# Attention sums of a graph layer: two of sixteen tiles weighted on VectorE, rows loaded two rounds ahead

## The chip, the cores and the metric
The kernel runs on one core of a Trainium2 chip. The metric is the device time of one execution in microseconds (us). The engines are TensorE (PE in the profile; its weight loads are PEld), VectorE (DVE), ScalarE (ACT), GpSimd (POOL) and SyncE (SP), which issues DMAs. Each engine runs its own stream of instructions in order; they meet only at semaphores, counters that an instruction raises when it is done and that another engine waits for.

## What is computed
Four layers follow one another on a graph of 3125 nodes and 53125 directed edges (sorted by their destination): graph attention, a mixture of experts, a five-layer graph convolution, and a second mixture of experts. The change touches one stage of the graph attention only, its last three lines:

```
h = (x @ W.T).reshape(n, H, D)                 # H = 8 heads of D = 32
h_src = h[src]
alpha = (h_src . a_src) + (h_dst . a_dst) + (enc . h_dst), leaky relu 0.2
ex = exp(alpha - segment_max(alpha, dst)[dst])
attn = ex / segment_sum(ex, dst)[dst]
out = segment_sum(h_src * attn[..., None], dst)   # this stage
return out.reshape(n, H * D) + bias
```

So every edge's row of 256 numbers (8 heads of 32) is multiplied by that edge's 8 attention weights, and the weighted rows of all edges with the same destination are added up.

## The kernel before
The stage is the function attention_sums. Edges are handled in tiles of 128 (one edge for each partition); there are 416 tiles, in 26 rounds (ITERS) of 16 tiles (BODY). Tile j of a round goes through four steps, on four engines, and SP feeds them:

- **SP, rows (L885) and weights (L888).** The gathered rows of the edges lie in DRAM (e_rows). They come in quads of four tiles, 544 KB each, into at_g, which has room for one round. Quad v of the next round is loaded as soon as the four tiles of quad v of this round are weighted (semaphore weighted). The attention weights at_attn come in halves of a round, two rounds ahead.
- **POOL, product (L878).** at_msg = row times weight, 128x256, both operands and the result in SBUF. It waits for the rows, for the weights, and, before each even tile, for summed: the slot of at_msg (sixteen of them) must have been read by PE one round earlier. Each product raises weighted.
- **ACT, one-hot (L936, L941).** It builds for each tile the 128x128 matrix that says which edge goes to which node of a window of 128 nodes, a quad at a time.
- **PE, sums (L959).** Per pair of tiles: wait for the one-hots (hot), for both products (weighted), and for added, that is, DVE has taken over the results that lie in the same PSUM bank from one round earlier (there are eight banks, one for each pair). Then two 32-bit matmuls for each tile, each of which stands as two in the profile, so eight for a pair. The pair raises summed by 2.
- **DVE, adds (L975).** add_tile adds the 128x256 result of a tile from PSUM to the window of agg that starts at the tile's first node. Successive windows overlap, so each add waits for summed and also for added: the add before it must have finished. DVE works four tiles (LAG) behind the tile number of its loop. The function body handles one round; its first act is lagging_bases, which loads the sixteen window starts into registers (L162, L163). The first round is written out (`body(0, True)`), the other 25 are a loop of one round (L985, `dve.Fori(1, ITERS)`), and the last four adds are written out behind the loop.

PE is thus held by three rings of sixteen tiles: at_msg between POOL and PE, the one-hots between ACT and PE, and the PSUM banks between PE and DVE. The stages before and behind this one are separated from it by a barrier of all engines.

## Time and profile before
| | us |
|---|---|
| median of 3 runs | 4766.83 (4765.92 to 4767.99) |
| the profiled execution's own time | 4765.28 |
| its span (first to last instruction) | 4763.5 |
| this stage in it, first row load to last add | 706.5 to 1002.0 |

| engine | busy us | share of the span |
|---|---|---|
| PE | 3822.2 | 80% |
| PEld | 3231.1 | 68% |
| DVE | 3018.3 | 63% |
| POOL | 2904.6 | 61% |
| ACT | 2211.9 | 46% |

The shares are means over stages that differ widely, so they say little about one stage. The stage of the change is 6% of the span; of its lines the page lists POOL's product at 242.4 us busy (416 of them, 614 ns each), PE's matmuls at 236.8 us (1664, 292 ns each; they overlap), and DVE's adds at 175.6 us (416, 422 ns each). Busy time is that of the instructions; waiting and register work of an engine's sequencer is not in it. Which engine sets the pace has to be read from the order of the waits in the stage.

### The profile page before, as it was taken

Reading aid. Unit: us, or ns where it says so; the run is one execution under the profiler, and the core shown is the slowest. Engines: PE = TensorE matmul, PEld = TensorE weight load, DVE = VectorE, ACT = ScalarE, POOL = GpSimd, SP = SyncE. Lnnn points to the kernel's source line nnn. Section 1 sums busy time; section 2 is a strip of 40 time slices with the busy share of each in tenths; the row PEclk is TensorE's granted clock in tenths of the full one; section 3 lists DMA queues with packets and bytes.
Section 4 is the critical chain, followed back from the end, with each engine's and each line's share of the span. In section 5 each row is a group of like instructions: output and inputs, shape, how many; then the busy total and the mean of one; then the engine's idle time right before and its main releaser. Section 6 shows DMA issues by size and latency. Waiting matters only on the chain. (4 is left out here: it accounts for less than half of the span.)

```text
span 4763.5 us, 103541 instructions
## 1 busy us (share of the span) xinstructions
PE 3822.2 (80%) x21812; PEld 3231.1 (68%) x21813; DVE 3018.3 (63%) x7234; ACT 2211.9 (46%) x4854; POOL 2904.6 (61%) x3160
## 2 busy tenths in 40 slices
PE   6999908867999688878888778886888878887598
PEld 4666607756888577767777677775777767776465
DVE  5667676664222576776776767776777767777544
ACT  3222227632232356555565555564556546565221
POOL 3777709823333477766777477774777747776142
PEclk8999959968999899999999899998999989999599
DMA  6888828735665555554555455553555535554432
GB/s 216 252 255 255 246 72 233 209 96 190 191 203 144 158 158 164 160 152 141 162 161 162 132 154 161 158 166 125 161 158 165 163 124 158 164 159 138 136 119 70
DMA packets 401352, 784.98 MB, mean 165 GB/s; under 512 B 178781, under 2 KB 242385, under 8 KB 383657
## 3 DMA queue, kind: packets, MB, share of 16 engines
q1 hardware_dynamic: 256115, 409.00, 26.7%
q0 software_dynamic: 133728, 352.78, 26.0%
q10 hardware_dynamic: 11094, 19.50, 1.3%
q14 instruction: 378, 3.10, 0.2%
q8 instruction: 37, 0.61, 0.1%
HBM read 665.35 MB, written 113.43 MB: 163 GB/s over the span
## 5 line engine op out<-in xcount | busy, mean ns | idle before, releaser
L2450 POOL DMA_INDIRECT g_g<-xl_rows,src_all x1640 | 1557.7, 950 | 525.9 <-issue 427.5
L2475 PE MATMUL g_b<-g_we,g_ea 128*128 128x256 f32 x4160 | 1163.5, 404 | 427.9 <-DVE g_msg L2575 372.7
L2488 PEld LDWEIGHTS g_b<-g_onehot,g_msg 128*128 128x128 f32 x8320 | 1117.0, 197 | 120.7 <-DVE agg L2596 36.7
L2488 PE MATMUL g_b<-g_onehot,g_msg 128*128 128x128 f32 x8320 | 1138.0, 281 | 36.7 <-DVE agg L2596 22.0
L2475 PEld LDWEIGHTS g_b<-g_we,g_ea 128*128 128x128 f32 x4160 | 734.7, 197 | 577.2 <-DVE g_msg L2575 461.7
L2596 DVE TENSOR_TENSOR agg<-agg,g_b 128x256 f32 x2080 | 870.0, 418 | 284.3 <-issue 145.5
L2552 ACT ACTIVATE g_msg<-g_msg 128x512 f32<-128x512 f32 x1040 | 652.8, 628 | 790.7 <-DVE g_msg L2575 784.7
L2575 DVE TENSOR_TENSOR g_msg<-g_g,g_b 128x512 f32<-128x512 f32 x1040 | 712.2, 685 | 402.9 <-DMA g_g<-xl_rows,src_all 239.2
L2532 ACT ACTIVATE g_away<-iota_row,dst_rel 128x128 f32<-128x128 f32 x1040 | 406.0, 390 | 209.2 <-DMA g_g<-xl_table,src_all 134.9
L2450 POOL DMA_INDIRECT g_g<-xl_table,src_all x410 | 390.8, 953 | 166.3 <-issue 153.8
L521 POOL DMA_INDIRECT sc_g<-h_table,sc_idx x416 | 405.2, 974 | 133.0 <-issue 116.7
L2537 ACT ACTIVATE g_onehot<-g_away,pos_w,neg_w 128x128 f32<-128x128 f32 x832 | 410.5, 493 | 110.8
L553 PE MATMUL sc_pe_h<-ae_h_rows,sc_onehot 128*128 x1664 | 429.4, 402 | 39.3 <-DVE sc_prod L658 39.3
L553 PEld LDWEIGHTS sc_pe_h<-ae_h_rows,sc_onehot 128*128 128x128 f32 x1664 | 301.5, 191 | 127.1 <-issue 85.6
L2582 DVE TENSOR_SCALAR g_onehot<-iota_row,dst_rel,pos_w 128x128 f32<-128x128 f32 x832 | 299.0, 359 | 83.9 <-issue 62.9
L878 POOL TENSOR_TENSOR at_msg<-at_g,at_attn 128x256 f32<-128x256 f32 x416 | 242.4, 614 | 140.3 <-DMA at_g<-e_rows 109.8
L596 ACT ACTIVATE sc_enc<-sc_pe_e 128x512 f32<-128x512 f32 x208 | 118.8, 598 | 425.8 <-PE sc_pe_e L542 398.2
L959 PE MATMUL at_ps<-at_onehot,at_msg 128*128 128x128 f32 x1664 | 236.8, 292 | 84.4 <-POOL at_msg L878 41.5
L959 PEld LDWEIGHTS at_ps<-at_onehot,at_msg 128*128 128x128 f32 x1664 | 209.2, 200 | 111.9 <-POOL at_msg L878 86.5
L1958 POOL DMA_INDIRECT sum_d<-ex_y,ex_give x56 | 100.0, 1787 | 266.3 <-DVE ex_y L1915 160.2
L1869 ACT ACTIVATE ex_hid<-ex_hp,ex_b 128x256 f32<-128x256 f32 (+1 forms) x256 | 114.4, 447 | 301.6 <-PE ex_hp L1827 297.7
L975 DVE TENSOR_TENSOR agg<-agg,at_ps 128x256 f32 x416 | 175.6, 422 | 120.2 <-PE at_ps L959 79.5
(359 smaller groups left out, 4298.5 us busy)
## 6 DMA issues: line engine op xcount, KB each, us to landing
g_ea<-in_ea SPq DMA_DIRECT2D x260, 512.0 KB
ex_w<-in_f_w SPq DMA_DIRECT2D x80, 1024.0 KB, 6.6
e_rows<-sc_g SPq DMA_DIRECT2D x52, 1088.0 KB, 5.0
at_g<-e_rows SPq DMA_DIRECT2D x104, 544.0 KB, 4.6
g_fetched<-xl_rows SPq DMA_DIRECT2D x3072, 1.0 KB
g_g<-xl_rows,src_all POOLq DMA_INDIRECT x1640
sc_rel<-rel_row ACTq DMA_DIRECT2D x52, 256.0 KB, 4.9
g_fetched<-xl_table SPq DMA_DIRECT2D x768, 1.0 KB
```

Source lines behind the costliest of these rows:

```text
L521: nc.gpsimd.indirect_dma_start(out=g[:, j, :], out_offset=None, in_=k.h_table[:, :], in_offset=bass.IndirectOffsetOnAxis(ap=idx[:, q, j % ...
L553: last = nc.tensor.matmul(pe_h[u % HB][:, i, 0:HROW], onehot[:, q, b, (at + i) * P:(at + i + 1) * P], k.h_rows[:, bass.ds(blocks[2 * u + i ...
L959: last = nc.tensor.matmul(ps[u][:, at:at + P], msg[:, j, b * P:(b + 1) * P], onehot[:, j, :], start=True, stop=True)
L2450: nc.gpsimd.indirect_dma_start(out=g.g[:, j, 0:width], out_offset=None, in_=table[:, :], in_offset=bass.IndirectOffsetOnAxis(ap=k.src_all[ ...
L2475: last = nc.tensor.matmul(ep[u % EB][:, i * D:(i + 1) * D], g.ea[:, q, (at + i) * P:(at + i + 1) * P], g.we[:], start=True, stop=True)
L2488: last = nc.tensor.matmul(ps[u % (SB // 2)][:, at:at + P], g.msg[:, j, b * P:(b + 1) * P], g.onehot[:, j, :], start=True, stop=True)
L2532: nc.scalar.activation(g.away[:, j // 2 % 2, :], k.iota_row[:], ACT.Abs, bias=k.dst_rel[:, bass.ds(it * BODY + j, 1)], scale=-1.0).then_in ...
L2537: nc.scalar.activation(g.onehot[:, j, :], g.away[:, j // 2 % 2, :], ACT.Relu, bias=bias, scale=scale).then_inc(g.act_hot, 1)
L2552: nc.scalar.activation(m, m, ACT.Relu).then_inc(g.relu, 1)
L2575: nc.vector.tensor_tensor(g.msg[:, 2 * u:2 * u + 2, :], g.g[:, 2 * u:2 * u + 2, 0:D], ep[u % EB][:, 0:2 * D].rearrange("p (a d) -> p a d", ...
L2582: nc.vector.tensor_scalar(g.onehot[:, j, :], k.iota_row[:], k.dst_rel[:, at], weight, ALU.is_equal, ALU.mult).then_inc(g.hot, 1)
L2596: nc.vector.tensor_tensor(window, window, ps[u % (SB // 2)][:, i * D:(i + 1) * D] .rearrange("p (b n) -> p b n", b=K), ALU.add).then_inc(g ...
```

## The change
DVE takes over the product of tiles 4 and 12 of every round (BY_DVE); POOL does the other fourteen and skips these two. DVE does such a product eight tiles (V_AHEAD = HALF) ahead of the tile number of its loop: tile 12 at the start of loop step j = 4, and tile 4 of the next round at step j = 12; since its adds lag by four tiles, tile 12 is weighted just before the add of tile 0 of the same round, and tile 4 of the next round just before the add of tile 8. Each product on DVE waits for its rows, its weights and its slot of at_msg (summed), and raises a new semaphore by_dve, for which PE (at the pairs that hold tiles 4 and 12) and SP wait besides weighted.

at_g gets room for two rounds instead of one, with eight semaphores for the landed quads instead of four, and SP loads both first rounds at once, then always two rounds ahead. SP's stream is written out in full instead of being a loop. DVE's loop now has two rounds in its body; the first two rounds and the last two are written out, so eleven turns of two rounds remain.

```diff
--- before.py
+++ after.py
@@ -854,60 +854,64 @@
     nc, a = k.nc, k.a
     PAIRS, QUADS = BODY // 2, BODY // 4
     ROUNDS = 2
+    BY_DVE = (4, 12)
+    ON_POOL = BODY - len(BY_DVE)
+    V_AHEAD = HALF
+
+    def of_pool(j):
+        return j - sum(t < j for t in BY_DVE)
+
+    def of_dve(j):
+        return sum(t < j for t in BY_DVE)
+
     with ExitStack() as c:
         sem, sb, bank = makers(k, c, "at")
-        g = sb("g", [P, BODY, GROW])
+        g = sb("g", [P, ROUNDS, BODY, GROW])
         attn = sb("attn", [P, ROUNDS, BODY, HEADS])
         msg = sb("msg", [P, BODY, D])
         onehot = sb("onehot", [P, BODY, P])
         one = sb("one", [P, 1])
         away = sb("away", [P, 2, 4, P])
         ps = [bank(f"ps{u}") for u in range(PAIRS)]
-        rows_in = [sem(f"rows_in{v}") for v in range(QUADS)]
+        rows_in = [sem(f"rows_in{v}") for v in range(ROUNDS * QUADS)]
         attn_in = [sem(f"attn_in{n}") for n in range(2 * ROUNDS)]
-        weighted, unit, distance, hot, summed, added = map(sem, (
-            "weighted", "unit", "distance", "hot", "summed", "added"))
+        weighted, by_dve, unit, distance, hot, summed, added = map(sem, (
+            "weighted", "by_dve", "unit", "distance", "hot", "summed", "added"))
         block = c.enter_context(nc.Block())
 
         def rows_of(it, v):
 
             return k.e_rows[bass.ds(it, 1), :, 4 * v:4 * v + 4, :].rearrange("a p t c -> p (a t) c")
 
-        def product(r, j):
-
-            return nc.gpsimd.tensor_tensor(
-                msg[:, j, :].rearrange("p (h c) -> p h c", h=HEADS), head_cols(g[:, j, 0:HROW]),
+        def product(engine, r, j):
+
+            return engine.tensor_tensor(
+                msg[:, j, :].rearrange("p (h c) -> p h c", h=HEADS), head_cols(g[:, r, j, 0:HROW]),
                 attn[:, r, j, :].unsqueeze(2).broadcast_to([P, HEADS, HD]), ALU.mult)
 
         @block.sync
         def _(sp):
-            def load_rows(v, it):
-                sp.dma_start(g[:, 4 * v:4 * v + 4, :], rows_of(it, v)).then_inc(rows_in[v], 16)
+            def load_rows(r, v, it):
+                sp.dma_start(g[:, r, 4 * v:4 * v + 4, :], rows_of(it, v)).then_inc(rows_in[r * QUADS + v], 16)
 
             def load_attn(r, q, it):
                 sp.dma_start(attn[:, r, q * HALF:(q + 1) * HALF, :], tile_rows(k.attn_d, it * BODY + q * HALF, HALF)
                              ).then_inc(attn_in[2 * r + q], 16)
 
-            load_attn(0, 0, 0)
-            load_rows(0, 0)
-            load_rows(1, 0)
-            load_attn(0, 1, 0)
-            load_rows(2, 0)
-            load_rows(3, 0)
-            for q in range(2):
-                load_attn(1, q, 1)
-            with sp.Fori(0, ITERS // ROUNDS - 1) as turn:
-                for r in range(ROUNDS):
-                    it = turn * ROUNDS + r
-                    for v in range(QUADS):
-
-                        sp.wait_ge(weighted, it * BODY + 4 * (v + 1))
-                        load_rows(v, it + 1)
-                        if v % 2 == 1:
-                            load_attn(r, v // 2, it + ROUNDS)
-            for v in range(QUADS):
-                sp.wait_ge(weighted, (ITERS - 2) * BODY + 4 * (v + 1))
-                load_rows(v, ITERS - 1)
+            for r in range(ROUNDS):
+                for v in range(QUADS):
+                    if v % 2 == 0:
+                        load_attn(r, v // 2, r)
+                    load_rows(r, v, r)
+            for it in range(ITERS - ROUNDS):
+                r = it % ROUNDS
+                for v in range(QUADS):
+                    sp.wait_ge(weighted, it * ON_POOL + of_pool(4 * (v + 1)))
+                    if of_dve(4 * (v + 1)):
+                        sp.wait_ge(by_dve, it * len(BY_DVE) + of_dve(4 * (v + 1)))
+                    load_rows(r, v, it + ROUNDS)
+                    if v % 2 == 1:
+                        load_attn(r, v // 2, it + ROUNDS)
 
         @block.gpsimd
         def _(pool):
@@ -916,12 +920,13 @@
                     it = turn * ROUNDS + r
                     for j in range(BODY):
                         if j % 4 == 0:
-                            pool.wait_ge(rows_in[j // 4], it * 16 + 16)
+                            pool.wait_ge(rows_in[r * QUADS + j // 4], turn * 16 + 16)
                         if j % HALF == 0:
                             pool.wait_ge(attn_in[2 * r + j // HALF], turn * 16 + 16)
                         if j % 2 == 0:
                             pool.wait_ge(summed, it * BODY + j + 2)
-                        product(r, j).then_inc(weighted, 1)
+                        if j not in BY_DVE:
+                            product(nc.gpsimd, r, j).then_inc(weighted, 1)
 
         @block.scalar
         def _(act):
@@ -951,7 +956,9 @@
                     v = u // 2
                     if u % 2 == 0:
                         pe.wait_ge(hot, it * QUADS + u // 2 + 3)
-                    pe.wait_ge(weighted, it * BODY + 2 * u + 2)
+                    pe.wait_ge(weighted, it * ON_POOL + of_pool(2 * u + 2))
+                    if 2 * u in BY_DVE or 2 * u + 1 in BY_DVE:
+                        pe.wait_ge(by_dve, it * len(BY_DVE) + of_dve(2 * u + 2))
                     pe.wait_ge(added, it * BODY + 2 * u + 2)
                     for j in (2 * u, 2 * u + 1):
                         for b in range(K):
@@ -975,15 +982,39 @@
                 nc.vector.tensor_tensor(window, window, ps[j // 2][:, j % 2 * D:(j % 2 + 1) * D]
                                         .rearrange("p (b n) -> p b n", b=K), ALU.add).then_inc(added, 1)
 
-            def body(it, first):
+            def weight_tile(turn, r, j):
+
+                it = turn * ROUNDS + r
+                dve.wait_ge(rows_in[r * QUADS + j // 4], turn * 16 + 16)
+                dve.wait_ge(attn_in[2 * r + j // HALF], turn * 16 + 16)
+                dve.wait_ge(summed, it * BODY + j - j % 2 + 2)
+                product(nc.vector, r, j).then_inc(by_dve, 1)
+
+            def weight_ahead(turn, r, j, final):
+
+                wraps, at = divmod(j + V_AHEAD, BODY)
+                if at in BY_DVE and not (final and wraps):
+                    of_turn, of_round = (turn, r) if r + wraps < ROUNDS else (turn + 1, -ROUNDS + r)
+                    weight_tile(of_turn, of_round + wraps, at)
+
+            def body(turn, r, first, final=False):
+                it = turn * ROUNDS + r
                 bases = lagging_bases(k, dve, base_regs, it * BODY)
                 for j in range(BODY):
+                    weight_ahead(turn, r, j, final)
                     if j >= LAG or not first:
                         add_tile(it * BODY + j - LAG, (j - LAG) % BODY, bases[j])
 
-            body(0, True)
-            with dve.Fori(1, ITERS) as it:
-                body(it, False)
+            for j in range(V_AHEAD):
+                if j in BY_DVE:
+                    weight_tile(0, 0, j)
+            for r in range(ROUNDS):
+                body(0, r, r == 0)
+            with dve.Fori(1, ITERS // ROUNDS - 1) as turn:
+                for r in range(ROUNDS):
+                    body(turn, r, False)
+            for r in range(ROUNDS):
+                body(ITERS // ROUNDS - 1, r, False, r == ROUNDS - 1)
             for i, base in enumerate(lagging_bases(k, dve, base_regs[0:LAG], ET)):
                 add_tile(ET - LAG + i, BODY - LAG + i, base)
             dve.wait_ge(added, ET + BODY)
```

## Rows read from the trace of the kernel before

**Rows 1.** Windows: start:end and length, then each engine's busy us (and count).
```profile
core 0: us, PE busy (x) PEld busy (x) DVE busy (x) ACT busy (x) POOL busy (x), PEclk, DMA share, GB/s
707.00:747.00 40.00, 34.44 (x240) 30.71 (x240) 19.36 (x46) 35.26 (x94) 36.25 (x64) 0.88 0.94 261
747.00:989.50 242.50, 200.12 (x1408) 176.57 (x1408) 147.82 (x351) 160.99 (x426) 206.20 (x353) 0.96 0.75 203
```

**Rows 2.** Waits of 712 to 1002.1: who waited for whom, us in total, times, longest.
```profile
PEld at_ps L959 <- POOL at_msg L878: 86.5, 54, 39.9
DVE agg L975 <- PE at_ps L959: 79.5, 145, 8.0
...
PE at_ps L959 <- DVE agg L975: 37.1, 22, 1.7
POOL at_msg L878 <- PE at_ps L959: 30.5, 28, 1.7
```

**Rows 3.** Timeline of DVE, loop: start, length, what, times [idle before].
```profile
754.30 0.98 DVE L975 TENSOR_TENSOR agg<-agg,at_ps 128x256 f32 x2 [0.20 <-PE at_ps L959]
757.17 0.98 DVE L975 TENSOR_TENSOR agg<-agg,at_ps 128x256 f32 x2 [1.89 <-PE at_ps L959]
```

**Rows 4.** Timeline of PE and of POOL, 843 to 862.
```profile
847.04 9.36 PE L959 MATMUL at_ps<-at_onehot,at_msg 128*128 128x128 f32 x64 [1.74 <-DVE agg L975]
...
848.25 9.41 POOL L878 TENSOR_TENSOR at_msg<-at_g,at_attn 128x256 f32<-128x256 f32 x16 [1.68 <-PE at_ps L959]
```

**Rows 5.** Timeline of POOL, 700 to 762.
```profile
710.75 51.69 POOL L878 TENSOR_TENSOR at_msg<-at_g,at_attn 128x256 f32<-128x256 f32 x90 [109.81 <-DMA at_g<-e_rows]
```

**Rows 6.** Timeline of DVE, adds outside the loop: first round, then the last.
```profile
714.21 0.42 DVE L975 TENSOR_TENSOR agg<-agg,at_ps 128x256 f32 x1 [8.01 <-PE at_ps L959]
...
715.91 0.42 DVE L975 TENSOR_TENSOR agg<-agg,at_ps 128x256 f32 x1 [0.65 <-PE at_ps L959]
...
717.42 0.42 DVE L975 TENSOR_TENSOR agg<-agg,at_ps 128x256 f32 x1 [0.47 <-PE at_ps L959]
...
721.78 0.42 DVE L975 TENSOR_TENSOR agg<-agg,at_ps 128x256 f32 x1 [0.20 <-PE at_ps L959]
723.83 0.98 DVE L975 TENSOR_TENSOR agg<-agg,at_ps 128x256 f32 x2 [1.63 <-PE at_ps L959]
...
999.75 0.42 DVE L975 TENSOR_TENSOR agg<-agg,at_ps 128x256 f32 x1 [0.47 <-DVE agg L975]
1000.37 0.42 DVE L975 TENSOR_TENSOR agg<-agg,at_ps 128x256 f32 x1 [0.20 <-DVE agg L975]
```

**Rows 7.** Line L162 (register loads), 715 to 990: count, ns min/median/max.
```profile
L162 DVEq TENSOR_LOAD <-base_lag x25: 1097/1102/1139, 722.0 to 988.3; - x25
```

**Rows 8.** Timeline of DVE: L1651 has two SBUF operands.
```profile
4539.41 0.42 DVE L1651 TENSOR_TENSOR ex_y<-ex_y,ex_xr 128x256 f32<-128x256 f32 x1
4539.75 0.42 DVE L1644 TENSOR_TENSOR ex_y<-ex_yp,ex_b 128x256 f32<-128x256 f32 x1
```

**Rows 9.** Timeline of DVE in a later stage: a free instruction behind adds.
```profile
2501.42 0.97 DVE L2596 TENSOR_TENSOR agg<-agg,g_b 128x256 f32 x2
2502.30 0.34 DVE L2582 TENSOR_SCALAR g_onehot<-iota_row,dst_rel,pos_w 128x128 f32<-128x128 f32 x1
```

**Rows 10.** Timeline of DVE and POOL, 4491 to 4495: two SBUF operands on both.
```profile
4491.17 0.33 DVE L1442 TENSOR_TENSOR st_hi_hot<-iota_row,st_hi 128x160 f32<-128x160 f32 x1
...
4492.31 0.59 POOL L1430 TENSOR_TENSOR st_value<-st_hi_hot,weight 128x160 f32<-128x160 f32 x1 [6.44 <-DVE st_lo_hot L1444]
4492.51 0.58 DVE L1442 TENSOR_TENSOR st_hi_hot<-iota_row,st_hi 128x160 f32<-128x160 f32 x1
```

**Rows 11.** Line L885, issues of 706 to 709.28: count, ns, and landing times.
```profile
L885 SPq DMA_DIRECT2D at_g<-e_rows x4: 424/560/580, 706.5 to 708.7; - x4
...
DMA to landing us min/median/max: 4.0/5.4/7.3
```

**Rows 12.** Timeline of PEld in a later stage: one pair of tiles, no wait.
```profile
2503.22 1.08 PEld L2488 LDWEIGHTS g_b<-g_onehot,g_msg 128*128 128x128 f32 x8
```

## The prediction

> **What bounds the stage now.** Read first the windows of the stage [rows 1]. In the long middle stretch (747 to 989.5 us) PE is busy 200 of 242 us, POOL 206, DVE 148: by busy time DVE comes last. The waits [rows 2] seem to agree: the largest sum is PE's weight loads waiting for POOL's products, 86.5 us. Both readings mislead, and the timelines show why. PE sits idle 1.74 us once a round, and what ends it is an add of DVE at the ring of PSUM banks; POOL then sits idle 1.68 us, ended by PE [rows 4]. So POOL waits for PE, and PE for DVE. DVE has the same gap, 1.89 us once a round [rows 3]; it is put down to PE, but PE had summed that tile long before (it is a ring of sixteen tiles ahead and itself waits for the next add). In this gap DVE's sequencer jumps back in its loop and loads sixteen window starts into registers, 1.10 us each time, 25 times [rows 7].
>
> DVE's beat is a chain: an add may start only when the one before it is done. Two adds take 0.98 us, so the second starts 0.55 us after the first, and the next pair starts 1.17 to 1.18 us after this one, which leaves 0.62 us between the pairs [rows 3]. Eight pairs are 9.4 us, and the step from a round's last add (754.85) to the next round's first (757.17) is 2.32 us in place of 0.62. Round: 9.4 + 1.7 = 11.1 us. POOL alone needs 51.69/90 = 0.574 us a tile, which it held until 762 us without a stop [rows 5], or 9.2 us a round; a pair on PE without a wait needs about 1.1 us at most [rows 12], or 8.6 us. DVE is the bound from its first add at 714.21 on, with only two short waits for PE in the first round [rows 6]. Whatever is put on DVE lengthens the stage, unless it fits into a gap of the chain; what is taken from POOL is taken from slack.
>
> **The parts of the change.**
>
> *POOL's two products fewer.* 2 x 0.574 us a round from an engine that already waits: worth 0.
>
> *DVE's two products more, the chain.* Such an instruction (both operands in SBUF, 256 numbers) lasts 0.42 us, and the next independent one starts 0.34 us after it [rows 8]. It always stands before an even tile, so in the 0.62 us step. It doesn't wait for the add in front of it, and it can start before that add has left the engine: a later stage has a free instruction 0.33 us after an add's start (the second add starts at 2501.97, the other at 2502.30) [rows 9]. Then product and next add are at 0.34 and 0.68 us: 0.06 more than 0.62. That is the low end. The three waits with their register work that the product brings along stand in front of it on DVE's sequencer; if they end only 0.1 us after the add is over, the next add starts at 0.42 + 0.1 + 0.34 = 0.86: 0.24 more, the high end. I take 0.15, nearer to the middle since some of that work fits under the running add. 50 products (52 less the two of the start, below) x 0.15 = 7.5 us (3 to 12).
>
> *The same, against POOL.* In a later stage DVE and POOL both run products with SBUF operands [rows 10]. L1442 takes 0.33 us alone; started at 4492.51, while POOL's L1430 ran from 4492.31 to 4492.90, it takes 0.58 and ends 0.19 us behind POOL's end. DVE was held until POOL had finished. DVE's adds read one operand from PSUM and show nothing of this: 0.42 us beside a POOL that never rests. The Trainium skill (SBUF — State Buffer, section "SBUF: two separate sides") says that VectorE instructions with two SBUF inputs and GpSimd instructions that read SBUF take one shared port pair in turns, for a whole instruction at a time. The trace agrees with it (0.58 against 0.33 us); that rule speaks against this change, since a product on POOL and one on DVE can't run side by side, and it makes the hold that I price here a standing cost rather than an accident.
>
> How often does it bite? PE can't pass tile 12 before DVE has weighted it, so PE now runs in bursts of four pairs: from product 12 to tile 4 of the next round, and so on. Let product 12 end at time 0. PE sums its pairs by about 1.1, 2.1, 3.1, 4.1 us [rows 12]; POOL, released by each of them, works from 1.2 to 1.8 and then from 2.2 to 5.7 us (six products at 0.574). DVE does eight adds (4.7 us) and comes with its next product at about 4.4: POOL is in the middle of one. The wait is what is left of it, between 0 and 0.5 us, and I take 0.25. In the other half round DVE has the round's end as well, comes at about 6 us, and finds POOL at rest. So 25 x 0.25 = 6.3, and 0.7 for the first three rounds, in which POOL never rests [rows 5]: 7 us (0 to 25 if all fifty waited 0.5).
>
> *Start.* DVE's first add (714.21) now stands behind product 12 of round 0, which needs the last quad. That quad was issued at 708.7 and took up to 7.3 us to land [rows 11]: 716.0. Plus 0.1 (an estimate) for the semaphore, 0.34 for the product, 0.25 for POOL: first add at 716.7, 2.5 us later. The two waits for PE that DVE then no longer meets were (0.65 - 0.20) + (0.47 - 0.20) = 0.7 us [rows 6]. Net +1.8 (0 to 3). If that quad lands later because eight are now asked for at once, this grows; they are queued behind it, so I add nothing.
>
> *DVE's loop of two rounds.* A step between rounds that is written out or lies inside the body has no jump: 723.83 - 721.78 = 2.05 us [rows 6] in place of 2.32. Of the 25 such steps, 24 were jumps and 10 will be: 14 x 0.27 = 3.7 us less (2 to 5). Against that, adds that are written out stand 0.62 us apart, each of them (1000.37 - 999.75) [rows 6], where every second one in the loop took 0.55. 48 more tiles are written out: 24 x 0.07 = 1.7 us more.
>
> *Rows two rounds ahead, SP written out.* POOL waited for rows once, at the start [rows 5]; nothing later hangs on them, so they are worth 0. They are also what keeps DVE from waiting: DVE needs tile 12's rows while the slot of the round before may still be in use. With one room DVE would meet that wait; with two, SP is released by DVE's product a round and a half before DVE needs the rows, some 17 us, against a landing of 7.3 at most [rows 11]. PE's and SP's new wait for by_dve: PE stops there once in each half round, as above, with the loads and matmuls of the following pair queued behind it; DVE is then eight adds from wanting them. Five more semaphores to clear behind the stage: 0.1 us, left out.
>
> **Sum.** 1.8 + 7.5 + 7 + 1.7 - 3.7 = 14.3 us on the profiled execution's 4765.3 us: 4779.6. The median of the runs shown is 1.5 us above that execution, so 4781.
>
> **Rivals.**
> 1. *The hold by POOL never costs* (DVE comes just as POOL ends a product, or goes between). For it: the phase of 4.4 us is uncertain by a whole product. Against it: rows 10. Then 1.8 + 7.5 + 1.7 - 3.7 = 7.3: 4774.
> 2. *POOL keeps its turn until its burst is over*, 5.7 in place of 4.4 us less the part that any start hides: 1.1 us, 25 times. Nothing shows two POOL products in a row with DVE waiting. 1.8 + 7.5 + 27.5 + 1.7 - 3.7 = 34.8: 4802.
> 3. *The loop of two rounds costs register work.* If its adds also stand 0.62 us apart each, 22 rounds x 8 x 0.07 = 12.3 more: 4793. The written-out adds show that the 0.55 isn't assured.
> 4. *Faster: POOL was the bound after all*, as the sum of 86.5 us has it. Then a round loses two products, 26 x 2 x 0.588 (9.41 us for 16 in rows 4) = 30.6 us, and the time is 4736. It decides if POOL's 1.68 us of idling is part of its own pace; against it stands that POOL ran 90 products at 0.574 without one. The Trainium skill (GPSIMD Engine Reference, section "Key points") calls VectorE about twice as fast for elementwise work, and by that rule the trade looks good; the trace agrees in size (a step of 0.34 against 0.574), but a faster product on the engine that sets the pace is still an addition.
>
> **Chances.** Forecast (4776.4 to 4790) 0.50; rival 1 with its neighbours (4765 to 4776.4) 0.25; rival 2 0.10; rival 3 0.08; rival 4 0.03, and 0.04 for a gain by cheaper steps in DVE's chain than I read. A measurement of this kernel tells about 0.2%, 9.5 us, from no change. Slower by more than that: 0.50 + 0.10 + 0.08 = 0.68; within it: 0.25 and half of the last 0.04 = 0.27; faster: 0.05. The range of 8 in 10 runs from 4768 (no hold, products nearly free) to 4801, just short of rival 2.
>
> **What would show it.** In the profile after: DVE's rounds at 11.1 + 12.5/26 = 11.6 us on average, with no wait for PE before an add; the products at two kinds of length, 0.42 us (tile 12) and longer where POOL runs (tile 4), with the next add starting shortly before such a product ends; POOL and PE idle longer than before, POOL's busy time down by 52 products; steps between rounds of 2.05 us inside the body. If DVE waits for PE or for rows behind the first round, or if POOL's idle time shrinks, my reading of the bound is wrong. If tile 4's products last 0.42 like tile 12's, the hold is.

## The result, and the profile after

The changed kernel takes 4773.4 us (median of 20 runs, 4768.8 to 4778.7) against 4766.7 us before (20 runs beside it): a ratio of 1.0013, with a 95% interval of 1.0007 to 1.0019. It is 6.7 us slower: less than the 14 us forecast, and on the side forecast. It lies in the prediction's range for 8 in 10 runs (4768 to 4801), near its lower end, but outside the band given 0.50 and within the 0.2% that the prediction had called no change and given only 0.27.

The two profiled executions lie 13.5 us apart (spans 4763.5 and 4777.0); that of after is the slowest of its twenty runs. Part of that is not the change: the stage starts 2.9 us later in the second one, at code that is the same in both, and 2.9 us more come behind it. So from here on the stage alone is compared, from DVE's memset to the end of its last add. It took 295.9 us before (706.14 to 1002.03) and 303.6 us after: 7.7 us more, which goes with the 6.7 of the medians.

The windows of after, for the stretches of [rows 1]:

```profile
core 0: us, PE busy (x) PEld busy (x) DVE busy (x) ACT busy (x) POOL busy (x), PEclk, DMA share, GB/s
707.00:747.00 40.00, 26.74 (x198) 26.19 (x199) 20.21 (x47) 30.53 (x81) 33.07 (x56) 0.80 0.93 305
747.00:989.50 242.50, 179.41 (x1388) 173.19 (x1386) 161.94 (x386) 163.89 (x435) 180.70 (x304) 0.93 0.69 198
```

In the middle stretch POOL is busy 181 us where it was 206, PE 179 where it was 200, and DVE 162 where it was 148. The work taken from POOL became rest, and the work given to DVE became length. PE's work is the same: before, it went through eight pairs at DVE's pace in 9.36 us [rows 4]; now it rests and then works in bursts, at a full clock four pairs in 3.83 us. The waits of the stage say who rests for whom (as [rows 2]):

```profile
PEld at_ps L966 <- DVE agg L982: 79.0, 37, 2.9
PE at_ps L966 <- DVE at_msg L888: 72.2, 37, 2.7
POOL at_msg L888 <- PE at_ps L966: 64.4, 71, 2.6
```

POOL waits 64 us for PE (30.5 before), and the line with POOL as releaser, first of [rows 2], is gone. The first two lines are one set of 37 gaps, seen by PE's weight loads and by its matmuls, and put down to different releasers. All 37 end 0.13 us after the end of a product on DVE, so it is the products that PE waits for. The two kinds of product, in count, ns (min, median, max) and form:

```profile
L888 POOL TENSOR_TENSOR at_msg<-at_g,at_attn x364: 606/617/875, 713.9 to 994.6; 128x256 f32<-128x256 f32 x182
L888 DVE TENSOR_TENSOR at_msg<-at_g,at_attn x52: 418/553/941, 715.2 to 1002.0; 128x256 f32<-128x256 f32 x52
```

And DVE's timeline in the loop, to be read beside [rows 3]:

```profile
881.85 0.97 DVE L982 TENSOR_TENSOR agg<-agg,at_ps 128x256 f32 x2 [0.20 <-DVE agg L982]
882.74 0.56 DVE L888 TENSOR_TENSOR at_msg<-at_g,at_attn 128x256 f32<-128x256 f32 x1
883.22 0.96 DVE L982 TENSOR_TENSOR agg<-agg,at_ps 128x256 f32 x2
884.38 0.98 DVE L982 TENSOR_TENSOR agg<-agg,at_ps 128x256 f32 x2 [0.20 <-DVE agg L982]
886.85 0.97 DVE L982 TENSOR_TENSOR agg<-agg,at_ps 128x256 f32 x2 [1.49 <-PE at_ps L966]
888.02 0.97 DVE L982 TENSOR_TENSOR agg<-agg,at_ps 128x256 f32 x2 [0.20 <-DVE agg L982]
888.91 0.42 DVE L888 TENSOR_TENSOR at_msg<-at_g,at_attn 128x256 f32<-128x256 f32 x1
889.25 0.96 DVE L982 TENSOR_TENSOR agg<-agg,at_ps 128x256 f32 x2
```

The product of 888.91 lasts 0.42 us, starts 0.34 us after the add in front of it (888.57) and has the next add 0.34 us behind it: a step of 0.68 in place of 0.62. That of 882.74 lasts 0.56: it was held, and the add behind it came 0.14 us later still. At 886.85 a round begins inside the loop's body, after 1.49 us of idling where the loop before had 1.89. The profile puts this idling down to PE; all of DVE's waits for PE over 0.2 us in the stage are of this kind, between rounds, where DVE's own register loads run.

From the starts of all 416 adds in each trace, the stage's 7.7 us split as follows (us):

| term | forecast | measured |
|---|---|---|
| first add later (8.07 to 9.91 after the memset) | +2.5 | +1.8 |
| other steps: waits for PE gone, more adds written out | -0.7 + 1.7 | +0.8 |
| 50 products, their length in the chain (0.674 - 0.622 each) | +7.5 | +2.6 |
| 50 products, held by POOL (50 steps of 42.2 in all, less 50 x 0.674) | +7 | +8.5 |
| 26 steps between rounds (58.5 to 52.5) | -3.7 | -6.0 |
| sum | +14.3 | +7.7 |

### The profile page after: what moved, and what is told of

Its sections match the earlier page's. It is cut to its first block and busy times, and to the rows that moved or that the text cites. A ratio compares the mean times of both kernels' runs of the same rounds, so it can differ in the third digit from the quotient of the medians.

```text
span 4777.0 us, 103318 instructions
## 1 busy us (share of the span) xinstructions
PE 3804.5 (80%) x21812; PEld 3239.6 (68%) x21813; DVE 3030.2 (63%) x7286; ACT 2210.7 (46%) x4854; POOL 2884.6 (60%) x3108
## 5 line engine op out<-in xcount | busy, mean ns | idle before, releaser
L888 POOL TENSOR_TENSOR at_msg<-at_g,at_attn 128x256 f32<-128x256 f32 x364 | 216.8, 628 | 174.4 <-DMA at_g<-e_rows 109.9
L966 PE MATMUL at_ps<-at_onehot,at_msg 128*128 128x128 f32 x1664 | 218.7, 297 | 112.3 <-DVE at_msg L888 72.2
```

Source lines behind the costliest of these rows:

```text
L966: last = nc.tensor.matmul(ps[u][:, at:at + P], msg[:, j, b * P:(b + 1) * P], onehot[:, j, :], start=True, stop=True)
```

## The experiments

Each kernel's stage is measured like the two above, in one profiled execution; a ratio is given where the kernel was timed in several rounds against the kernel before on the same chip.

**The loop without the products (loop_only).**

```diff
-    BY_DVE = (4, 12)
+    BY_DVE = ()
```

> The changed kernel with no tile on DVE: POOL weights all sixteen, everything else (two-round loop, two rounds of rows, SP written out) stays. The stage is counted from DVE's memset to the end of its last add: 295.9 us before, 303.6 after. Theory (DVE's chain is the bound): the steps between rounds stay as short as after (6.0 us less than before), the written-out adds cost about 1.5 us, the products' 11.1 us and the later first add (1.8 us) are gone: stage 291.4 us, time 4.5 us below before. Rival (only the saved jumps count, 14 x 0.27 us): stage 293.7 us. Rival (POOL is the bound, so giving it back two tiles a round costs): stage above 303.6 us.

Measured: stage 292.4 us; time 4763.6 us against 4766.3, ratio 0.9994 (0.9985 to 1.0003). The first theory holds to 1 us. The half of the change that rewrites DVE's loop gains 3.5 us of stage, and the half that moves work to DVE costs 11.2. Giving the two tiles back to POOL cost nothing, so POOL isn't the bound. The steps at a jump and inside the body:

```profile
842.33 0.97 DVE L982 TENSOR_TENSOR agg<-agg,at_ps 128x256 f32 x2 [0.20 <-PE at_ps L966]
845.19 0.98 DVE L982 TENSOR_TENSOR agg<-agg,at_ps 128x256 f32 x2 [1.88 <-PE at_ps L966]
...
853.42 0.98 DVE L982 TENSOR_TENSOR agg<-agg,at_ps 128x256 f32 x2 [0.20 <-PE at_ps L966]
855.91 0.97 DVE L982 TENSOR_TENSOR agg<-agg,at_ps 128x256 f32 x2 [1.52 <-PE at_ps L966]
```

From the second add of 842.33 (842.89) to 845.19 it is 2.30 us at the jump, and from 853.98 to 855.91 it is 1.93 inside the body.

**POOL silent (pool_counts).**

```diff
+            for j in range(BODY):
+                nc.gpsimd.memset(msg[:, j, :], 1.0).then_inc(filled, 1)
+            pool.wait_ge(filled, BODY)
...
                         if j not in BY_DVE:
-                            product(nc.gpsimd, r, j).then_inc(weighted, 1)
+                            pool.sem_inc(weighted, 1)
...
+                if isinstance(turn, int) and turn == 0:
+                    dve.wait_ge(filled, BODY)
```

> The changed kernel with POOL's products left out: POOL fills its slots once with ones and then only counts, so the sums of fourteen tiles in sixteen are not the reference's. DVE's 52 products stay. Theory (the lengths above 0.42 us are POOL's hold): all products behind the first ones last 0.42 us, the 8.5 us of hold go, stage 295.1 us apart from its start. Rival (the long ones are DVE's own, from waits or operands): lengths up to 0.94 us stay, stage 303.6 us.

POOL fills its slots with ones once and then only counts, so this kernel leaves out fourteen of the sixteen products of a round.

```profile
L888 DVE TENSOR_TENSOR at_msg<-at_g,at_attn x52: 417/418/426, 714.4 to 993.3; 128x256 f32<-128x256 f32 x52
```

All 52 products last 0.42 us (417 to 426 ns, against 418 to 941 in after), and the stage is 295.4 us: 8.2 us less than after, against 8.5 us of hold added up from its steps. So the long products were held by POOL's products.

**How long a hold is.** Five kernels with products on both engines (four_tiles, one_room, at_round_end, one_at_end, four_and_two), and the changed kernel itself, give 228 products of DVE that were started while one of POOL ran. In 224 of them the rule is the same to within 0.015 us: DVE's product lasts 0.42 us plus what was left of POOL's, less 0.14, and nothing if less than 0.14 us was left. The one product of [rows 10] fits it too: 0.33 + 0.39 - 0.14 = 0.58. POOL's next product is held in its turn (up to 0.875 us in the row above, where it took 0.617). The Trainium skill (SBUF — State Buffer, section "SBUF: two separate sides") says that whichever of the two starts first has the shared ports for the whole instruction and the other fully blocks; the trace agrees in these 224, but for the last 0.14 us, which cost DVE nothing. In the other four DVE missed its turn (at_round_end, below).

**Four tiles (four_tiles).**

```diff
-    BY_DVE = (4, 12)
+    BY_DVE = (4, 6, 12, 14)
```

> The changed kernel with four tiles a round on DVE (4, 6, 12, 14) in place of two. Theory: 0.05 us in the chain for each product (50 more: 2.6 us) and a hold by POOL of the same size for each product (0.17 us: 8.5 us), less if POOL, with twelve tiles, rests more: stage 309 to 315 us. Rival (the hold is a matter of POOL's load alone and fades): stage 306 us. Rival (POOL was the bound and is relieved): stage below 303.6 us.

Measured: stage 308.0 us, 1 us below the theory's range and 2 above its rival. 101 steps with a product sum up to 76.2 us: 101 x 0.674 = 68.1 for the chain, 8.1 of hold (the median of the 57 steps whose product was not held is 0.674 again). So the chain's price is the same for each product (0.05 us), but the hold is not: 101 products lost as much as 50 had, 0.08 us each. With twelve tiles POOL is busy 153 of 242 us in the middle stretch, and a product meets it less often. This expectation was half wrong: a hold can't be costed per product, only from how busy the other engine is and when.

**One room for the rows (one_room).**

```diff
-        g = sb("g", [P, ROUNDS, BODY, GROW])
+        g = sb("g", [P, BODY, GROW])
...
-            for it in range(ITERS - ROUNDS):
+            for it in range(ITERS - 1):
...
-                    load_rows(r, v, it + ROUNDS)
+                    load_rows((it + 1) % ROUNDS, v, it + 1)
```

> The changed kernel with rows for one round only in SBUF, as before the change: a quad is loaded for the next round once POOL and DVE have weighted this round's. Theory A (as the prediction said): DVE meets a wait for rows before its products, visible as idle time before them, stage several us above 303.6. Theory B (PE and POOL are more than half a round ahead of the add, so a landing of 5 to 7 us is covered): no wait, stage 303.6 us give or take 2, and the second room is worth nothing.

```profile
PE at_ps L967 <- DVE at_msg L888: 70.3, 37, 2.9
POOL at_msg L888 <- DMA at_g<-e_rows: 50.7, 58, 2.4
...
DVE at_msg L888 <- DMA at_g<-e_rows: 8.6, 2, 5.6
```

Measured: stage 301.9 us, no longer than after. POOL now waits for rows 58 times behind its start, 50.7 us in all, but DVE only twice, at the start, as in after. Theory B holds. The second room takes real waits away, all of them from an engine with time to spare.

**The products between the rounds (at_round_end).** If a product costs only what it adds to the chain, it should be free in the long step between rounds.

```diff
-    BY_DVE = (4, 12)
+    BY_DVE = (8, 12)
...
             def body(turn, r, first, final=False):
                 it = turn * ROUNDS + r
+                for at in BY_DVE:
+                    weight_tile(turn, r, at)
                 bases = lagging_bases(k, dve, base_regs, it * BODY)
                 for j in range(BODY):
-                    weight_ahead(turn, r, j, final)
```

> DVE still weights two tiles a round (8 and 12), but both products stand at the start of a round, in front of the register loads, where DVE's sequencer is busy for over 1 us anyway. Theory (a product costs only what it adds to the chain): the products vanish under the register loads, stage as loop_only plus about 1.5 us for the later first add, 292.9 us, time 3 us below before. Rival (a product costs its own length and POOL's hold wherever it stands): stage about 303 us.

Measured: stage 310.0 us, time 4780.6 us, ratio 1.0028 (1.0018 to 1.0039). The theory missed by 17 us. Three things came: the steps between rounds are 2.30 us inside the body and 2.75 at the jump (loop_only: 1.94 and 2.31), which is 24 x 0.4 = 9.6 us; the first add is 3.3 us later; and one step of the second round is 7.9 us long. That one is here, with POOL's own timeline:

```profile
724.78 0.42 DVE L982 TENSOR_TENSOR agg<-agg,at_ps 128x256 f32 x1 [0.20 <-DVE agg L982]
725.11 7.62 DVE L888 TENSOR_TENSOR at_msg<-at_g,at_attn 128x256 f32<-128x256 f32 x2
732.66 0.41 DVE L982 TENSOR_TENSOR agg<-agg,at_ps 128x256 f32 x1
...
711.07 21.05 POOL L888 TENSOR_TENSOR at_msg<-at_g,at_attn 128x256 f32<-128x256 f32 x36 [109.73 <-DMA at_g<-e_rows]
```

The first of the two products began at 725.11 and lasted 7.29 us. Its rows and weights had landed: POOL had already taken tiles 9 and 10, of the same quad and the same half round. POOL did twelve products in that time without letting it in, and stopped at 732.12 only because PE, waiting for this very product, no longer freed slots.

**The same waits without the products (waits_end, waits_mid).** Here POOL weights all sixteen tiles, and of DVE's weight_tile only the waits are left.

```diff
-                        if j not in BY_DVE:
-                            product(nc.gpsimd, r, j).then_inc(weighted, 1)
+                        product(nc.gpsimd, r, j).then_inc(weighted, 1)
...
-                product(nc.vector, r, j).then_inc(by_dve, 1)
+                dve.sem_inc(by_dve, 1)
```

> at_round_end with its two products taken out and their waits kept, in front of the register loads. Theory (the time between rounds is that of DVE's sequencer, and the waits of two tiles add some 0.4 us of sequencer work to it, whether a product follows or not): steps between rounds 2.3 us inside the body and 2.7 us at a jump, as in at_round_end, stage 303 to 306 us; the one hold of 7.3 us is gone. Rival (the products or POOL's hold made these steps long): steps as in loop_only, 1.94 and 2.31 us, stage 294 to 297 us.

> The changed kernel with DVE's two products a round taken out and their three waits kept where they stand: POOL weights all sixteen tiles, DVE only waits and counts by_dve. Theory (the waits fit under the running add; the product itself costs the chain 0.05 us and POOL's hold the rest): all steps before an even tile 0.62 us, stage 293 to 294.5 us (loop_only's 292.4 plus the later start). Rival (the 0.05 us is the waits' own): steps of 0.67 us there, 296.5 us.

waits_end (the edit on at_round_end): stage 308.5 us, steps of 2.47 and 2.92 us.

```profile
851.84 0.97 DVE L981 TENSOR_TENSOR agg<-agg,at_ps 128x256 f32 x2 [0.20 <-PE at_ps L965]
855.31 0.97 DVE L981 TENSOR_TENSOR agg<-agg,at_ps 128x256 f32 x2 [2.49 <-PE at_ps L965]
...
863.53 0.98 DVE L981 TENSOR_TENSOR agg<-agg,at_ps 128x256 f32 x2 [0.20 <-PE at_ps L965]
866.56 0.97 DVE L981 TENSOR_TENSOR agg<-agg,at_ps 128x256 f32 x2 [2.05 <-PE at_ps L965]
```

From 852.39 to 855.31 it is 2.92 us and from 864.08 to 866.56 it is 2.48, without any product. So the long steps of at_round_end come from its waits on DVE's sequencer, which stand in line with the jump and the register loads. Here they are 0.17 us longer still than in at_round_end, and the stage lies above the expected 303 to 306. The difference between the two is a count (sem_inc) of its own in place of each product, which raises the semaphore itself; that the counts take the 0.17 us is likely, not shown apart.

waits_mid (the edit on the changed kernel): stage 293.7 us. Of the 50 steps that have the waits in them 39 are 0.62 us, and 11 are 0.68: those with the waits for tile 4 of the loop's next turn. This execution ran at a mean granted TensorE clock of 0.725 (0.923 in after) and took 5086.3 us, so only DVE's steps are used from it. In the middle of the chain the same waits cost nothing or, in these 11, 0.06 us; most of them fit under the running add. With a product in the step and POOL silent, 49 of the 50 are 0.67 to 0.68, the 11 too (pool_counts). So what a product there costs, 0.05 us and its hold, is the product's own.

**One product between the rounds (one_at_end).**

```diff
-    BY_DVE = (8, 12)
+    BY_DVE = (8,)
```

> at_round_end with one product a round (tile 8) in place of two. Theory (sequencer work): half of the 0.4 us a round, 0.2 us x 24, and a start like loop_only's plus 1 to 2 us: stage 298 to 300 us if the long hold in the second round does not come. Whether it comes: at_round_end had one product of 7.29 us while POOL did twelve in a row. If that needs two products behind one another on DVE it is gone here; if it is a matter of when DVE asks for its turn, it can come again.

```profile
722.60 9.86 DVE L888 TENSOR_TENSOR at_msg<-at_g,at_attn 128x256 f32<-128x256 f32 x1
732.38 0.41 DVE L982 TENSOR_TENSOR agg<-agg,at_ps 128x256 f32 x1
...
719.51 12.66 POOL L888 TENSOR_TENSOR at_msg<-at_g,at_attn 128x256 f32<-128x256 f32 x22
```

Measured: stage 307.3 us, steps of 2.13 and 2.58 us (0.2 and 0.3 above loop_only, as expected), and the long hold came again, 9.86 us for a single product, with sixteen products of POOL in a row inside it. So it doesn't need two products behind one another. What it needs stays open: both long holds are at the end of the first round, while POOL never rests; but the changed kernel's products in that stretch got in after one product of POOL, and the moment of asking, 0.21 and 0.48 us into a product of POOL's, lies where others were let in. Three of the four that missed a turn asked within the last 0.14 us of a product of POOL's with the next right behind it, but fifteen others did so too and lost nothing.

**Shortening the chain itself (bases_by_pair, bases_by_four).** If DVE's chain is the bound, the 1.7 us between rounds is where the time is. Both kernels are the kernel before with that part alone changed: the window starts are loaded behind the dispatch of an add, two or four at a time. This is the edit of bases_by_four:

```diff
+            def load_bases(tile, group):
+                dve.load(base_regs[4 * group:4 * group + 4], k.base_lag[0:1, bass.ds(tile, 4)])
+            def held(group):
+                return [dve.snap(reg, min_val=0, max_val=N) for reg in base_regs[4 * group:4 * group + 4]]
...
-                bases = lagging_bases(k, dve, base_regs, it * BODY)
-                for j in range(BODY):
-                    if j >= LAG or not first:
-                        add_tile(it * BODY + j - LAG, (j - LAG) % BODY, bases[j])
+                for j in range(LAG if first else 0, BODY):
+                    if j % 4 == 0:
+                        bases = held(j // 4)
+                    add_tile(it * BODY + j - LAG, (j - LAG) % BODY, bases[j % 4])
+                    if j % 4 == 1:
+                        load_bases(it * BODY + j + 3, (j // 4 + 1) % 4)
```

> The kernel before with one edit: the sixteen window starts are not loaded at once between rounds but two at a time, behind the dispatch of an add and thus under it. POOL keeps all tiles. Theory (DVE's chain with its 1.7 us between rounds is the bound): most of 25 x 1.7 us goes, less some 0.1 us for each pair: stage 270 us (265 to 280), time some 25 us below before. Rival (POOL or PE is the bound and DVE's gap is slack): stage stays at 290 us or above.

> The kernel before with one edit: window starts are loaded four at a time, behind the dispatch of an add, instead of sixteen at once between rounds. A load of two took 0.53 us in bases_by_pair and stood eight times in a round; the load of four behind the loop of the kernel before took 0.35 us, which an add of 0.42 us nearly covers. Theory (DVE's chain is the bound, and the cost is what sticks out of the add): about 0.1 us for each of four loads and 0.2 us for the jump in place of 1.7 us a round, DVE's round 10.0 us in place of 11.1, stage 268 us (262 to 278), time 28 us below before. Rival (a load under a running add is slow whatever its size, 0.5 us and more): the step behind each load is 0.3 to 0.4 us longer, stage 290 us or above. Rival (POOL at 9.2 us a round is the bound from here): no shorter than 250 us, so it could not be seen.

The loads of the two kernels (count, ns min, median, max):

```profile
L162 DVEq TENSOR_LOAD <-base_lag x194: 523/529/575, 729.6 to 1039.9; - x194
...
L980 DVEq TENSOR_LOAD <-base_lag x99: 340/343/383, 720.9 to 967.6; - x99
```

bases_by_pair: stage 341.3 us, time 4813.7 us, ratio 1.0098 (1.0083 to 1.0113): 45 us worse instead of 25 better. A load of two takes 0.53 us, longer than the add of 0.42 that was to cover it, and with its register work the step inside a pair grew from 0.55 to 0.96 us, eight times a round: 207 such steps cost 84 us, and the shorter steps between rounds gave 38 back. So the expectation failed on the load's time, which had been guessed at about 0.1 us outside the add; that longer work on DVE lengthened the stage, with POOL and PE unchanged, fits DVE as the bound. bases_by_four: stage 270.8 us (expected 268), time 4738.0 us against 4765.8, ratio 0.9944 (0.9930 to 0.9957). A load of four takes 0.34 us. The theory holds, and the rival of 290 us is out.

```profile
861.14 0.97 DVE L975 TENSOR_TENSOR agg<-agg,at_ps 128x256 f32 x2 [0.20 <-DVE agg L975]
862.43 0.98 DVE L975 TENSOR_TENSOR agg<-agg,at_ps 128x256 f32 x2 [0.31 <-PE at_ps L959]
863.80 0.98 DVE L975 TENSOR_TENSOR agg<-agg,at_ps 128x256 f32 x2 [0.40 <-DVE agg L975]
865.11 0.97 DVE L975 TENSOR_TENSOR agg<-agg,at_ps 128x256 f32 x2 [0.33 <-DVE agg L975]
```

A load sticks out of its add by 0.11 us (861.14 to 862.43 is 1.29 in place of 1.175), and from the last add of a round (862.98) to the first of the next (863.80) it is 0.82 us where the kernel before had 2.32. Why four registers load faster than two, the runs don't say.

**Both together (four_and_two, four_no_product).** The changed kernel with the same loads of four, and that with `BY_DVE = ()`.

> The changed kernel (DVE weights tiles 4 and 12, two rounds in the loop) with the same loads of four. Theory: against bases_by_four it adds the products' 0.05 us each in the chain, their hold by POOL (0.17 us each in the changed kernel, more here because POOL rests less: 0.3 us), and 1.8 us at the start: 3 + 15 + 2 = 20 us more, less some 3 us for fewer jumps: stage 17 us above bases_by_four. Rival (with DVE's chain shortened POOL becomes the bound, so taking two tiles from it pays): stage below bases_by_four.

> four_and_two with no tile on DVE: loads of four window starts, two rounds in the loop, all sixteen products on POOL. Theory: 11 jumps of 0.2 us are saved against bases_by_four and 48 written-out tiles cost 1.7 us, so stage 270 us (268 to 272), and what four_and_two (291.7 us) has above it are its two products a round: 50 x (0.05 + 0.35 to 0.44 us of hold) and the start. Rival (two rooms of rows, the written-out SP or the longer loop cost something of their own with the shorter chain): stage 275 us or above.

```profile
L888 DVE TENSOR_TENSOR at_msg<-at_g,at_attn x52: 418/779/878, 713.1 to 988.6; 128x256 f32<-128x256 f32 x52
```

four_and_two: stage 291.7 us, 20.9 above bases_by_four where 17 were expected, time 4759.6 us, ratio 0.9986 (0.9976 to 0.9995). four_no_product: stage 268.0 us (expected 268 to 272), time 4738.5 us, ratio 0.9941 (0.9928 to 0.9955). Nothing but the two products a round lies between them, and they cost 23.7 us of stage here where they cost 11.2 on the longer chain. The 50 steps with a product sum up to 53.0 us against 31.1 without one: 2.6 for the chain and 19 of hold and of waits sticking out. The median product takes 0.78 us, because POOL, with DVE faster, hardly rests. The fastest version is one of the two with loads of four and all products on POOL; their intervals overlap.

## Why the prediction was right or wrong

**The bound was right.** DVE's chain set the pace, and the ring of waits had told it where the largest sums of [rows 2] had not: POOL idles more after than before, and shortening DVE's step between rounds gave 28 us at once with POOL's work unchanged (bases_by_four). The round came to 11.3 us on average where 11.6 was named as a sign.

**The chain's price was right in kind and three times too large** (2.6 us where 7.5 stood, below the range of 3 to 12). The term that was mis-sized is the middle value of 0.15 for a product: its three waits were taken to stick out of the running add in part. Measured was 0.05: the waits fit under the add but for 0.06 us in 11 of 50 steps, which the product itself covers (waits_mid, pool_counts), and the product starts 0.34 us after the add, as the free instruction of [rows 9] did after 0.33. That row had given 0.06, close to what came.

**The hold was right in size (8.5 against 7), in part by luck, and wrong in place.** The prediction had it bite tile 4's products, 25 x 0.25 = 6.3 us, and behind the first three rounds never tile 12's. The 25 products of tile 4 cost 3.9 us, and the 25 of tile 12 cost 4.6: one part was too large, and another that had been put at nothing made up for it. The step that failed is that PE always works in bursts of four pairs. Between its first and its last burst it did 24 of four pairs in after and 12 of eight:

```profile
878.55 3.83 PE L966 MATMUL at_ps<-at_onehot,at_msg 128*128 128x128 f32 x32 [2.60 <-DVE at_msg L888]
883.43 3.83 PE L966 MATMUL at_ps<-at_onehot,at_msg 128*128 128x128 f32 x32 [1.05 <-DVE at_msg L888]
889.46 9.03 PE L966 MATMUL at_ps<-at_onehot,at_msg 128*128 128x128 f32 x64 [2.20 <-DVE at_msg L888]
...
894.11 6.36 POOL L888 TENSOR_TENSOR at_msg<-at_g,at_attn 128x256 f32<-128x256 f32 x11 [0.33 <-PE at_ps L966]
```

What tells the two apart is TensorE's granted clock, which the prediction left out. The windows of the second and the third burst (the third number from the end is the mean granted clock, 1.00 and 0.61):

```profile
883.40:887.40 4.00, 3.83 (x32) 3.65 (x32) 1.92 (x6) 2.94 (x9) 3.41 (x7) 1.00 0.80 210
889.40:893.40 4.00, 3.94 (x22) 3.95 (x23) 2.88 (x8) 0.80 (x2) 1.43 (x3) 0.61 0.75 194
```

All 24 bursts of four ran at the full clock: four pairs take 3.83 us, DVE's next product starts 4.2 us after the burst's start or later and ends at 4.6 or later, and PE has run dry. In each of the twelve of eight the granted clock stood at its lower level, half of full, for 3.4 us, beginning between 0.4 us before and 1.3 us behind the start; PE had just rested for 2.2 to 2.7 us, but it had rested as long before bursts at the full clock too. Four pairs then take 5.2 to 5.3 us, DVE's product is there before PE asks for it, and PE goes on to the eighth pair. POOL follows with up to eleven products in a row (894.11 to 900.47) and is still busy when DVE comes with tile 12's at 900.09. Eleven of the twelve products of tile 12 behind a burst of eight were held, 4.1 us in all; behind the third round none of the eleven behind a burst of four was. The other kernels agree: one_room has 24 bursts of four and 12 of eight, four_tiles 20 and 14, four_and_two 47 and none, and in each the lower clock stands in every burst of eight and in none of four. No run was made with the clock held at one level, so this is read from the order of events and not from an experiment.

The bounds of 0 to 0.5 us for one hold were read well from [rows 10] (one of 0.52 was seen); the mean of 0.25 was too high for tile 4's, 0.15 measured. Rival 1 (no hold, 4774) came out nearest in time, and its mechanism is refuted (pool_counts). Rival 2, POOL keeping its turn for a whole burst, never happened in the profile of after, where a single turn was missed (0.52 us, at 753.19), but it did in at_round_end and one_at_end: it is a real mechanism and a rare one.

**The steps between rounds gained 6.0 us where 3.7 stood.** The term was mis-sized by reading 2.05 us from [rows 6] for every step without a jump. That row is the entry into the loop, and the step at the entry was 2.05 again in after (737.98 + 2.05 = 740.03). A step inside the body takes 1.92 and a written-out one 1.79, while the jumps stayed at 2.30.

**The start** was 1.8 us for 2.5: the first add came behind product 12, which waited for its rows, as forecast. **The second room for rows** was worth nothing to the bound, as forecast, but the claim that DVE would wait for rows without it was wrong (one_room).

**Rivals 3 and 4** fell: the loop's adds keep their 0.55 and 0.62 us (the median inside a pair is 0.553 in both kernels), and POOL was not the bound (loop_only).

The chances, finally, were set from a forecast that was too far up by two terms. The chain's price from its nearest row (50 x 0.06 = 3.0 in place of 7.5) would have brought the sum from 14.3 to 9.8 us. The other 2.3 us, of the steps between rounds, no row of before had shown: it has no step inside a body of two rounds. With them it is 7.5, beside 7.7 measured in the stage; that this agrees so well also rests on the luck with the hold.

## What to carry to other kernels

Find the bound by following a ring of waits round, not by the largest sum of waiting: an engine's idle time put down to another may be its own register loads and jumps, and these are the first thing to shorten. An instruction added to a chain of dependent ones costs little where it and its waits fit under a running one, and its full sequencer time where the sequencer is what is late. Before work is moved between VectorE and GpSimd, see whether both read two operands from SBUF; then they take turns, and the price grows as the other engine fills. The price also hangs on when the other engine is busy, and a third engine's pauses and clock can decide that.

## What was not expected of the hardware

- A product of DVE asked for while POOL ran one was let in after it in 224 of 228 cases, at the cost of the rest of POOL's less 0.14 us. In two it missed one turn (0.5 us), and in two it waited for 12 and 16 products of POOL in a row (7.29 and 9.86 us). When it misses its turn is open.
- A register load on DVE takes 0.53 us for two registers, 0.34 for four and 1.10 for sixteen.
- A wait on DVE that is already met still takes time when nothing runs over it: the waits of two tiles and their counts made a step between rounds 0.5 to 0.6 us longer (waits_end), and the same waits under an add nothing or 0.06 us (waits_mid).
- In after PE rests 37 times in the stage, for 0.9 to 2.7 us, and its granted clock stood at the lower level in ten spells of 3.4 us in the middle stretch (747 to 989.5), where before had five. PE was no bound in either, but its slower bursts moved POOL's work to where it held DVE.
